# Loads of fold factors at the start of a graph-network kernel, and the place of a fold's last split quarter

## The chip, the cores and the metric

The kernel runs on one core of a Trainium2 chip. The time is that of the device in microseconds, from the launch of the program to its end. A core has a matrix engine (PE, TensorE), three engines for elementwise work (DVE, the vector engine; ACT, the scalar engine; POOL, GpSimd), and SP, which issues transfers (DMAs). Each runs its own list of instructions in order, and they wait for each other by semaphores. Tiles lie in SBUF with up to 128 partitions; matmuls write to PSUM (`ps`), which has eight banks.

## What is computed

The reference takes 625 nodes with 512 features and 20625 edges and runs four graph layers. Cut to what matters here:

```python
    # layer L1: three rounds of mean aggregation in both directions
    for l in range(3):
        h_self = h
        fwd_neigh = _mean_agg(h, src, dst, n) @ W_fwd[l].T
        bwd_neigh = _mean_agg(h, dst, src, n) @ W_bwd[l].T
        cat = jnp.concatenate((h_self, fwd_neigh, bwd_neigh), axis=1)
        h = jax.nn.relu(cat @ W_self[l].T)
...
    # layer L0, over all edges (sorted by the kernel first)
    edge_feature = jax.nn.silu(edge_rbf @ We1 + be1) @ We2 + be2
    msg = edge_feature * x[col]
    agg = jax.ops.segment_sum(msg, row, num_segments=N_NODES)
```

In L1, `W_fwd[l]` and `W_bwd[l]` are each followed by a 512-column part of `W_self[l]`, with nothing but a matrix product between. The kernel multiplies these weights together beforehand: three rounds with two directions make six products of two 512x512 matrices, the fold products.

## The kernel before

**Stages.** The first 140 us or so prepare two things side by side. One is the six fold products (`FOLDS` = 6). The other is a sort of the edges into slots of 128 by the chunk of their source node. Then the edge loop of layer L0 runs (83 steps), and then the node layers. The prediction speaks of the first part and of the start of the edge loop.

**A fold product.** Product m has the factors `fold_a[m]` and `fold_b[m]`, 1 MB each, loaded by `load_factors(m)` on SP into the tile `stage0` or `stage1`, by turns (m % 2). The product has four quarters (m,0) to (m,3), each with its own PSUM bank: `fold(m, u)` on PE. ACT copies each quarter out (`product_out`, line L695, tile `folded`), and SP stores the whole product to memory (`save_product`).

The first three products (m < `WHOLE` = 3) are taken straight from `stage` in float32: 8 records of about 0.43 us each (L1050). The last three are split first. ACT rounds a quarter of both factors to `fold_hi` (`factor_high`, L680), DVE takes the rest as `fold_lo` (`factor_low`, L1575), and PE runs three fast matmuls for each (L997 to L999). A quarter of the splitting is a quarter of the summed index, and every quarter (m,u) of the product sums over all four. So (m,0) needs all four splits, one after the other, and the others need none that is new. `stage0`, `fold_hi0` and `fold_lo0` lie in one region of SBUF, those with number 1 in another.

**The sorting columns.** The sort is a scatter by matmul. There are 28 groups of columns, each with 6 columns (the last has 3). For each group DVE builds `hot_lo`, `hot_hi` (L1563) and `ended` (L1569), ACT builds `keyed` (`mark`, L688) out of `hot_lo`, and PE adds them up (`place`, L1035 and L1038). The tiles of a group form a ring of four, so a group waits until PE is done with the one four before.

**What sets the order.** It is written out by hand. The table `AFTER[m][u]` gives the groups that PE places behind `fold(m, u)`: one or two behind each from (1,0) to (3,3), none behind (4,1) and later. ACT and DVE walk through the same quarters. In the step of (m,u) they first do the columns of the groups that PE needs behind the next quarter, then split quarter u of the factors of product m + 1, and ACT then copies out (m,u). In (2,1) the layer norm of x lies between, and in (4,1) the tables of the sort.

**The queue of SP.** The transfers go out in the order of the code, with waits between. Factors m + 2 can be loaded when product m no longer reads the buffer: m = 2, 3, 4 wait for PE (`fold_mm`), and m = 5 waits for the splitting of product 3 (`split_lo`). Between stand the stores of the products and of `h32` (the normed input, to `h_dram`), and the weights of the edge loop.

**Behind the products.** When the last quarter of product 5's factors is split, DVE still does the low half of the edge weights (`we_lo`, L1582), tables (L1587 to L1646), `rT_lo` (L1654), two memsets (L1720, L1721) and `s_lo` (L1660). PE runs the edge loop's first matmuls between and behind (5,2) and (5,3).

## Time and profile before

| | us |
|---|---|
| median of 3 runs | 1199.06 |
| the three runs | 1197.98, 1199.06, 1199.83 |
| the profiled execution | 1200.69 |
| its span, first to last instruction | 1198.9 |
| PE busy | 1158.1 (97% of the span) |
| DVE busy | 851.5 (71%) |
| ACT busy | 680.5 (57%) |
| mean granted clock of PE | 0.989 |

The profiled execution is one run of the program; all durations are from it. A line of a timeline gives the start, the time taken, engine, line, operation, the output and input tiles with their shapes, and in brackets how long the engine had stood still and what released it. Several instructions of a kind in a row are one line (x6). Times are counted from the start of the span. Matmuls overlap, so a matmul's own duration is longer than the distance between two starts.

### The profile page before, as it was taken

What the parts mean: (1) busy time and instruction counts of PE and PEld (TensorE: products, weight loads), DVE (VectorE), ACT (ScalarE), POOL (GpSimd) and SP (SyncE); (2) the same over time, 40 slices, a digit from 0 to 9 for tenths busy, and PEclk for the clock granted to TensorE, in tenths of its full rate; (3) what the DMA queues carried; (4) which work ended last, traced back from release to release, by engine and by line L of the source; (5) the groups of instructions that cost most, each with busy time, mean ns of one, the idle gap of its engine ahead of it and who ended that gap; (6) DMA issues with size and microseconds to landing.
All of it is one profiled execution on the core that took longest, in us unless ns stands there. A gap on an engine that the chain in (4) does not pass through costs nothing.

```text
span 1198.9 us, 20918 instructions
## 1 busy us (share of the span) xinstructions
PE 1158.1 (97%) x6268; PEld 970.2 (81%) x6268; DVE 851.5 (71%) x1479; ACT 680.5 (57%) x1351; POOL 418.6 (35%) x546
## 2 busy tenths in 40 slices
PE   6989899999999999999999999998899999999997
PEld 3658788888888888888888888886789888798786
DVE  8767777777777777777777777777977234175664
ACT  3567567676676766767676676765734223142352
POOL 2001555565546555555555555551500000001000
PEclk9999999999999999999999999999899999999999
DMA  5544622222222222222222322221101202022101
GB/s 192 205 154 158 234 87 72 83 82 71 87 74 79 80 74 85 70 85 77 76 85 68 87 74 79 82 72 36 44 1 37 71 8 97 0 71 71 44 2 44
DMA packets 26966, 95.88 MB, mean 80 GB/s; under 512 B 6533, under 2 KB 6783, under 8 KB 22578
## 3 DMA queue, kind: packets, MB, share of 16 engines
q0 software_dynamic: 18592, 54.42, 15.2%
q1 hardware_dynamic: 8208, 40.84, 9.5%
q8 instruction: 23, 0.38, 0.1%
q10 hardware_dynamic: 130, 0.13, 0.0%
q14 instruction: 13, 0.11, 0.0%
HBM read 86.52 MB, written 8.85 MB: 80 GB/s over the span
## 4 chain that ended last, share of the span: by engine, by line
PE 88%; DVE 6%; ACT 3%; issue 1%; DMA 1%; DVEq 0%; SPq 0%; ACTq 0%
PE ps L1004 13%; PE ps L1006 12%; PE ps L1005 12%; PE ps L997 9%; PE ps L999 9%; PE ps L998 9%; PE ps L1012 3%; PE ps L1011 3%; PE ps L1111 3%; PE ps L1110 3%; PE ps L1050 3%; PE ps L1115 2%; PE ps L1038 1%; PE ps L1247 1%; PE ps L1065 1%
## 5 line engine op out<-in xcount | busy, mean ns | idle before, releaser
L1004 PE MATMUL ps<-we_hi,s_hi 128*128 128x512 f32 x664 | 268.7, 405 | 0.0
L1006 PE MATMUL ps<-we_hi,s_lo 128*128 128x512 f32 x664 | 260.2, 392 | 0.0
L1005 PE MATMUL ps<-we_lo,s_hi 128*128 128x512 f32 x664 | 260.1, 392 | 0.0
L578 POOL DMA_INDIRECT xg<-h_dram,node_picks x166 | 177.0, 1066 | 96.7 <-POOL node_picks L568 66.1
L720 ACT ACTIVATE m_hi<-msg 128x512 fp32r<-128x512 f32 x166 | 105.0, 632 | 156.9 <-DVE msg L1667 92.9
L572 POOL DMA_INDIRECT rbf<-in_edge,edge_picks x166 | 171.5, 1033 | 50.5 <-issue 33.5
L1672 DVE TENSOR_TENSOR m_lo<-msg,m_hi 128x512 fp32r<-128x512 f32 x166 | 114.9, 692 | 59.3 <-ACT m_hi L720 58.6
L1660 DVE TENSOR_TENSOR s_lo<-s,s_hi 128x1024 fp32r<-128x1024 f32 x83 | 101.8, 1226 | 75.5 <-ACT s_hi L714 50.3
L1006 PEld LDWEIGHTS ps<-we_hi,s_lo 128*128 128x128 f32 x664 | 124.9, 188 | 28.6
L1005 PEld LDWEIGHTS ps<-we_lo,s_hi 128*128 128x128 f32 x664 | 125.7, 189 | 21.1
L1004 PEld LDWEIGHTS ps<-we_hi,s_hi 128*128 128x128 f32 x664 | 125.3, 189 | 21.4
L710 ACT ACTIVATE s<-ps,be 128x256 f32<-128x256 f32 x332 | 129.6, 478 | 2.9 <-PE ps L999 2.9
L1667 DVE TENSOR_TENSOR msg<-ps,xg 128x512 f32<-128x512 f32 x166 | 113.5, 684 | 0.0
L997 PE MATMUL ps<-rT_hi,we_hi 128*128 128x256 f32 x332 | 102.7, 309 | 3.8 <-issue 2.7
L723 ACT ACTIVATE ps<-row_a 128x512 f32<-128x512 f32 x166 | 97.0, 584 | 0.1
L999 PE MATMUL ps<-rT_hi,we_lo 128*128 128x256 f32 x332 | 94.3, 284 | 0.0
L998 PE MATMUL ps<-rT_lo,we_hi 128*128 128x256 f32 x332 | 94.2, 284 | 0.0
L714 ACT ACTIVATE s_hi<-s 128x1024 fp32r<-128x1024 f32 x83 | 88.0, 1061 | 5.6
L630 POOL TENSOR_TENSOR diag<-adj_hi,adj_lo 125x125 f32<-125x125 f32 x5 | 2.1, 456 | 213.7 <-DVE w_lo L1901 213.7
L1702 DVE TENSOR_TENSOR acc_agg<-ps,acc_agg 125x512 f32 x80 | 55.3, 692 | 22.5 <-issue 22.0
L568 POOL COPY node_picks<-slot_dst 128x2 int32 (+1 forms) x83 | 15.2, 183 | 160.6 <-DVE msg L1667 160.6
L997 PEld LDWEIGHTS ps<-rT_hi,we_hi 128*128 128x128 f32 x332 | 63.8, 192 | 4.6 <-issue 3.1
(301 smaller groups left out, 2556.4 us busy)
## 6 DMA issues: line engine op xcount, KB each, us to landing
stage<-in_fold_a SPq DMA_DIRECT2D x6, 1024.0 KB, 5.1
stage<-in_fold_b SPq DMA_DIRECT2D x6, 1024.0 KB, 8.6
fold_dram<-folded SPq DMA_DIRECT2D x6, 1024.0 KB
wstage<-fold_dram SPq DMA_DIRECT2D x6, 1024.0 KB, 4.9
w_raw<-in_nodew SPq DMA_DIRECT2D x3, 1024.0 KB, 7.2
wstage<-in_selfw SPq DMA_DIRECT2D x3, 1024.0 KB, 5.0
rbf<-in_edge,edge_picks POOLq DMA_INDIRECT x166
xg<-h_dram,node_picks POOLq DMA_INDIRECT x166
```

Of the source, the lines that this page charges most:

```text
L572: pool.indirect_dma_start(rbf[t.slot][:, j], None, a["edge"], bass.IndirectOffsetOnAxis(ap=edge_picks[t.slot][:, j:j + 1], axis=0)).then_i ...
L578: pool.indirect_dma_start(xg[t.slot][:, j], None, h_dram, bass.IndirectOffsetOnAxis(ap=node_picks[t.slot][:, j:j + 1], axis=0)).then_inc(x ...
L710: act.activation(s32[:, u], ps[:, 1 + u // 2, (u % 2) * PAIR:(u % 2) * PAIR + PAIR], ACT.Silu, bias=be1[:, u:u + 1]).then_inc(silu_ready, 1)
L720: act.activation(m_hi[s][:, j], msg[j][:], ACT.Copy).then_inc(m_hi_ready, 1)
L997: pe.matmul(outp, lh, rh, start=start, stop=False)
L998: pe.matmul(outp, lh, rl, start=False, stop=False)
L999: return pe.matmul(outp, ll, rh, start=False, stop=stop)
L1004: pe.matmul(outp, lh, rh, start=False, stop=False, skip_group_check=True)
L1005: pe.matmul(outp, lh, rl, start=False, stop=False, skip_group_check=True)
L1006: return pe.matmul(outp, ll, rh, start=False, stop=False, skip_group_check=True)
L1667: dve.tensor_tensor(msg[j][:], ps[:, 3 + j], xg[s][:, j], op=ALU.mult).then_inc(msg_ready, 1)
L1672: dve.tensor_tensor(m_lo[s][:, j], msg[j][:], m_hi[s][:, j], op=ALU.subtract).then_inc(m_lo_ready, 1)
```

## The change

The factors of products 0, 1 and 2 no longer go to `stage`. They go to three tiles `plain0` to `plain2`, which take the places of `fold_hi1`, `fold_lo1` and `fold_hi0`; these are written only when products 0, 1 and 2 are done. `stage` is left to products 3, 4 and 5. SP issues the loads of products 0 to 4 at the start, with x between 1 and 2, and there is a semaphore for each product's load. The load of 5 still waits for the splitting of product 3, but now stands in front of the stores of `h32` and of products 2 and later. `factor_high` waits for `fold_mm` in every product that is split.

The second part moves the split of the last quarter (u == K - 1). On ACT and on DVE it now stands in front of the columns of that step, where it stood behind them.

```diff
+        plain_at = (spare.at - 2 * 2 * K * F * 4, spare.at - 2 * K * F * 4, pre.at - 2 * 2 * K * F * 4)
+        plain = [Region(at)(f"plain{m}", [P, 2, K, F], F32) for m, at in enumerate(plain_at)]
...
-        stage_in = [sem(f"stage_in{i}") for i in range(2)]
+        stage_in = [sem(f"stage_in{m}") for m in range(FOLDS)]
...
             def load_factors(m):
+                factors = plain[m] if m < WHOLE else stage[m % 2]
                 for part, w in enumerate((a["fold_a"], a["fold_b"])):
-                    sp.dma_start(stage[m % 2][:, part].rearrange("p k f -> p (k f)"), w[m]).then_inc(stage_in[m % 2], 16)
+                    sp.dma_start(factors[:, part].rearrange("p k f -> p (k f)"), w[m]).then_inc(stage_in[m], 16)
...
             load_factors(0)
             load_factors(1)
             sp.dma_start(x_res[:], a["x"].rearrange("(c p) f -> p c f", p=NC)).then_inc(x_in, 16)
-            sp.wait_ge(fold_mm, K)
-            load_factors(2)
+            for m in range(2, FOLDS - 1):
+                load_factors(m)
             save_product(0)
...
-            for m in range(3, FOLDS):
-                if m - 2 < WHOLE:
-                    sp.wait_ge(fold_mm, K * (m - 1))
-                else:
-                    sp.wait_ge(split_lo, K * (m - 1 - WHOLE))
-                load_factors(m)
-                save_product(m - 2)
-                if m == 4:
-                    sp.wait_ge(ln_act, 1 + C)
-                    sp.dma_start(h_dram.rearrange("(c p) f -> p c f", p=NC), h32[:]).then_inc(h_saved, 16)
-            for m in range(FOLDS - 2, FOLDS):
+            save_product(1)
+            sp.wait_ge(split_lo, K)
+            load_factors(FOLDS - 1)
+            sp.wait_ge(ln_act, 1 + C)
+            sp.dma_start(h_dram.rearrange("(c p) f -> p c f", p=NC), h32[:]).then_inc(h_saved, 16)
+            for m in range(2, FOLDS):
                 save_product(m)
...
             def factor_high(m, k):
-                act.wait_ge(stage_in[m % 2], 32 * (m // 2 + 1))
-                if m - 2 >= WHOLE:
-                    act.wait_ge(fold_mm, K * (m - 1))
+                act.wait_ge(stage_in[m], 32)
+                act.wait_ge(fold_mm, K * (m - 1))
...
             for n, (m, u) in enumerate(units):
+                if u == K - 1 and WHOLE <= m + 1 < FOLDS:
+                    factor_high(m + 1, u)
                 if n + 1 < len(units):
                     for i in AFTER[units[n + 1][0]][units[n + 1][1]]:
                         mark(i)
-                if WHOLE <= m + 1 < FOLDS:
+                if u < K - 1 and WHOLE <= m + 1 < FOLDS:
                     factor_high(m + 1, u)
...
-                        mm = pe.matmul(ps[:, 1 + u], stage[m % 2][:, 0, k, f], stage[m % 2][:, 1, k],
+                        mm = pe.matmul(ps[:, 1 + u], plain[m][:, 0, k, f], plain[m][:, 1, k],
...
+                if u == K - 1 and WHOLE <= m + 1 < FOLDS:
+                    factor_low(m + 1, u)
                 if n + 1 < len(units):
                     for i in AFTER[units[n + 1][0]][units[n + 1][1]]:
                         hots(i)
                 if (m, u) == (FOLDS - 2, 1):
                     slot_tables()
-                if WHOLE <= m + 1 < FOLDS:
+                if u < K - 1 and WHOLE <= m + 1 < FOLDS:
                     factor_low(m + 1, u)
```

On SP, the transfers from the first factors to the load of product 5 stand in this row before (`stage_134` and `stage_135` are stage0 and stage1, `folded_196` and `folded_197` the two tiles of finished products):

```order
3 L470 DMA stage_134<-in_fold_a 128x2048
4 L470 DMA stage_134<-in_fold_b 128x2048
5 L470 DMA stage_135<-in_fold_a 128x2048
6 L470 DMA stage_135<-in_fold_b 128x2048
7 L478 DMA x_res<-in_x 125x5x512
8 L470 DMA stage_134<-in_fold_a 128x2048
9 L470 DMA stage_134<-in_fold_b 128x2048
10 L474 DMA fold_dram<-folded_196 128x2048
...
20 L474 DMA fold_dram<-folded_196 128x2048
21 L495 DMA h_dram<-h_82 125x5x512
22 L470 DMA stage_135<-in_fold_a 128x2048
23 L470 DMA stage_135<-in_fold_b 128x2048
```

Of the change (`plain_140` to `plain_142` are plain0 to plain2, `folded_199` and `folded_200` the tiles of finished products):

```order
7 L482 DMA x_res<-in_x 125x5x512
8 L474 DMA plain_142<-in_fold_a 128x2048
9 L474 DMA plain_142<-in_fold_b 128x2048
10 L474 DMA stage_135<-in_fold_a 128x2048
11 L474 DMA stage_135<-in_fold_b 128x2048
12 L474 DMA stage_134<-in_fold_a 128x2048
13 L474 DMA stage_134<-in_fold_b 128x2048
14 L478 DMA fold_dram<-folded_199 128x2048
...
20 L474 DMA stage_135<-in_fold_a 128x2048
21 L474 DMA stage_135<-in_fold_b 128x2048
22 L494 DMA h_dram<-h_82 125x5x512
23 L478 DMA fold_dram<-folded_199 128x2048
```

The loads of products 3 and 4 have moved up behind that of 2, and the last load has moved in front of `h_dram` and the store of product 2.

On ACT, the steps of (2,2) and (2,3), where groups 17 to 20 are keyed and the last two quarters of product 3's factors split, before:

```order
34 L688 ACTIVATE keyed_189<-hot_lo_181,keys 125x256 x3
35 L688 ACTIVATE keyed_190<-hot_lo_182,keys 125x256 x3
36 L680 ACTIVATE fold_hi_137<-stage_135 128x2x512
37 L695 ACTIVATE folded_196<-ps 128x512
38 L688 ACTIVATE keyed_191<-hot_lo_183,keys 125x256 x3
39 L688 ACTIVATE keyed_188<-hot_lo_180,keys 125x256 x3
40 L680 ACTIVATE fold_hi_137<-stage_135 128x2x512
41 L695 ACTIVATE folded_196<-ps 128x512
```

And in the change:

```order
34 L686 ACTIVATE keyed_192<-hot_lo_184,keys 125x256 x3
35 L686 ACTIVATE keyed_193<-hot_lo_185,keys 125x256 x3
36 L678 ACTIVATE fold_hi_137<-stage_135 128x2x512
37 L693 ACTIVATE folded_199<-ps 128x512
38 L678 ACTIVATE fold_hi_137<-stage_135 128x2x512
39 L686 ACTIVATE keyed_194<-hot_lo_186,keys 125x256 x3
40 L686 ACTIVATE keyed_191<-hot_lo_183,keys 125x256 x3
41 L693 ACTIVATE folded_199<-ps 128x512
```

The second `fold_hi` has moved from behind the two `keyed` to in front of them; the same is done on DVE with `fold_lo`, and on both once more in the step of (3,3).

## Rows read from the trace of the kernel before

**Rows 1.** The page: busy time of each engine, share of the span, instructions.

```profile
PE 1158.1 (97%) x6268; PEld 970.2 (81%) x6268; DVE 851.5 (71%) x1479; ACT 680.5 (57%) x1351; POOL 418.6 (35%) x546
```

**Rows 2.** Waits, 0 to 140 us: waiting <- waited for: total us, times, longest.

```profile
PE ps L997 <- DVE fold_lo L1575: 4.4, 1, 4.4
...
PE ps L997 <- issue: 2.7, 1, 2.7
...
PE ps L997 <- DVE rT_lo L1654: 1.1, 1, 1.1
```

**Rows 3.** Timeline of PE: group 17, then starts in (3,0) to (4,0).

```profile
78.48 0.24 PE L1035 MATMUL ps<-hot_hi,keyed 125*128 125x166 f16 x1 [0.51 <-issue]
...
81.14 0.48 PE L997 MATMUL ps<-fold_hi 128*128 128x512 f32 x1
...
87.90 0.80 PE L997 MATMUL ps<-fold_hi 128*128 128x512 f32 x1 [4.44 <-DVE fold_lo L1575]
...
92.81 0.48 PE L997 MATMUL ps<-fold_hi 128*128 128x512 f32 x1
...
103.82 0.48 PE L997 MATMUL ps<-fold_hi 128*128 128x512 f32 x1
...
109.32 0.48 PE L997 MATMUL ps<-fold_hi 128*128 128x512 f32 x1
...
111.47 0.39 PE L997 MATMUL ps<-fold_hi 128*128 128x512 f32 x1
```

**Rows 4.** Timeline of ACT: first split of product 3, and around its last.

```profile
63.54 1.06 ACT L680 ACTIVATE fold_hi<-stage 128x1024 fp32r<-128x1024 f32 x1 [4.82 <-DMA stage<-in_fold_b]
...
80.42 0.58 ACT L695 ACTIVATE folded<-ps 128x512 f32<-128x512 f32 x1
...
84.34 1.30 ACT L688 ACTIVATE keyed<-hot_lo,keys 125x256 f16<-125x256 f16 x3 [0.69 <-DVE hot_lo L1563]
85.55 1.04 ACT L680 ACTIVATE fold_hi<-stage 128x1024 fp32r<-128x1024 f32 x1
```

**Rows 5.** Timeline of DVE: the splits of product 3, and the columns between.

```profile
80.55 1.22 DVE L1575 TENSOR_TENSOR fold_lo<-stage,fold_hi 128x1024 fp32r<-128x1024 f32 x1 [3.54 <-ACT fold_hi L680]
81.70 0.55 DVE L1563 TENSOR_TENSOR hot_lo<-iota_lo,lo 125x768 f16<-125x768 f16 x1
...
83.69 0.55 DVE L1563 TENSOR_TENSOR hot_lo<-iota_lo,lo 125x768 f16<-125x768 f16 x1
...
86.62 1.23 DVE L1575 TENSOR_TENSOR fold_lo<-stage,fold_hi 128x1024 fp32r<-128x1024 f32 x1 [0.85 <-ACT fold_hi L680]
87.76 0.55 DVE L1563 TENSOR_TENSOR hot_lo<-iota_lo,lo 125x768 f16<-125x768 f16 x1
```

**Rows 6.** Busy time by stretch; last three columns: PE's clock, DMA share, GB/s.

```profile
15.00:18.00 3.00, 3.00 (x7) 1.27 (x7) 2.93 (x5) 1.10 (x1) 0.00 (x0) 1.00 0.33 128
82.00:90.00 8.00, 3.56 (x15) 2.35 (x14) 7.15 (x14) 5.34 (x11) 0.00 (x0) 0.85 0.60 244
...
131.00:145.00 14.00, 11.33 (x56) 9.56 (x56) 8.64 (x9) 8.80 (x16) 6.71 (x7) 0.88 0.64 232
```

**Rows 7.** DMA issues: loads of folds 0, 1, 2, 5 (second halves); last, us to landing.

```profile
stage<-in_fold_b SPq DMA_DIRECT2D x1, 1024.0 KB, 7.4
...
stage<-in_fold_b SPq DMA_DIRECT2D x1, 1024.0 KB, 11.4
...
stage<-in_fold_b SPq DMA_DIRECT2D x1, 1024.0 KB, 8.7
...
stage<-in_fold_b SPq DMA_DIRECT2D x1, 1024.0 KB, 12.9
```

**Rows 8.** Timelines of ACT and DVE: copy of (4,2), last split quarter of product 5.

```profile
118.55 0.60 ACT L695 ACTIVATE folded<-ps 128x512 f32<-128x512 f32 x1 [0.84 <-PE ps L999]
...
120.13 1.23 DVE L1575 TENSOR_TENSOR fold_lo<-stage,fold_hi 128x1024 fp32r<-128x1024 f32 x1 [1.16 <-ACT fold_hi L680]
```

**Rows 9.** Timeline of SP: issue of fold 1's second half.

```profile
2.91 0.64 SPq L470 DMA_DIRECT2D stage<-in_fold_b  x1
```

More of the change, by code:

```diff
@@ L298, in build @@
         assert spare.at <= keep.at
+        plain_at = (spare.at - 2 * 2 * K * F * 4, spare.at - 2 * K * F * 4, pre.at - 2 * 2 * K * F * 4)
+        plain = [Region(at)(f"plain{m}", [P, 2, K, F], F32) for m, at in enumerate(plain_at)]
+        assert len(plain) == WHOLE
         ends16 = pre("ends16", [EP, 2, ETP], F16)
@@ L1044, in fold @@
                 if m < WHOLE:
-                    pe.wait_ge(stage_in[m % 2], 32 * (m // 2 + 1))
+                    pe.wait_ge(stage_in[m], 32)
                 if m > 0:
```

## The prediction

> **Notation.** (m,u) is quarter u of fold product m. "Group i" is the i-th of 28 groups of sorting columns. A quarter of a fold's factors is split by fold_hi on ACT and then fold_lo on DVE. Only the first 140 us of 1198.9 us matter; I take the later work as it is and shift it.
>
> **What bounds the kernel now.** I read the page's busy times first [rows 1]: PE is busy 97% of the span, so a gain is either PE work removed or PE idle time removed. The change removes no matmul. So I went to the waits of the first 140 us [rows 2] and looked for PE's idle time: 4.4 us in which a split matmul waited for fold_lo, 1.1 us for rT_lo, and 2.7 us of "issue". (What PE waits at the start for the counting of edges is not touched.)
>
> PE's timeline shows the big hole [rows 3]. (3,0) starts at 81.14 and could run its fourth quarter 2.15 us later (111.47-109.32, the same distance in (4,0)); it runs it at 87.90. A smaller hole, 0.51 us, lies in front of group 17 at 78.48. What came late is seen on ACT and DVE [rows 4, 5]: the fourth quarter's fold_hi ran at 85.55, behind groups 19 and 20 (the latter keyed at 84.34), and its fold_lo at 86.62 to 87.85. The granted clock of 82 to 90 us is 0.85 [rows 6]. So part of it ran at the lower of its two levels (1.2 instead of 2.4 GHz), behind a PE that had stood still for 4.4 us.
>
> Farther back, ACT started fold_hi of product 3's first quarter at 63.54, having stood still 4.82 us for the factors, so since 58.72 [rows 4]: they are issued only when PE has let go of their buffer. From there on DVE and ACT take 6.07 us for two groups and one quarter (81.70 to 87.76 [rows 5]), and everything they do hangs on that start.
>
> **Part 1, early loads.** The factors of folds 0 to 2 lie in places of their own and those of 3 and 4 are issued at the start. The bytes are the same, 2 MB a fold. The loads land one after the other, not together: fold 1's second half, issued at 2.9 us [rows 9], lands 11.4 us later at 14.3; fold 0's, issued a microsecond before it, takes 7.4 us, so it lands some 5 us sooner; that of fold 2 takes 8.7 us [rows 7]. So 2 MB more in the queue land 5 us later, 2.4 us a megabyte and at worst 8.7/2 = 4.4, and what stands behind does not slow what stands in front. x_res comes next; while it moves, the DMA share is 0.33 at 128 GB/s [rows 6], so its 1.25 MB take 10 us, to about 24 us. The 6 MB behind it take 6 x 2.4 = 14 us, 26 at worst: all there by 38 to 50 us. Needed: fold 3 at 58.7, fold 2 a few us sooner, fold 4 not before 84. All is covered, at cost 0. Whether so long a stretch of transfers slows DVE or ACT this trace does not show apart; hot_lo takes 0.55 us at 81.70, shortly behind a load, and at 87.76, during one [rows 5], so I take nothing.
>
> The gain: ACT starts (3,0)'s fold_hi at 58.72 instead of 63.54, 4.8 us sooner, and DVE and ACT keep that lead to (2,2), since nothing else holds them there. The added wait for fold_mm is no wait: ACT has by then copied out the product that it asks for. PE gets 0.51 us at once: group 17, for which it waited until 78.48 [rows 3], is ready, so (3,0) starts at 81.14-0.51 = 80.63.
>
> **Part 2, the last quarter in front of the columns.** The third quarter's fold_lo, 80.55 to 81.78 before, moves to 75.7 to 76.9. ACT's next fold_hi, the last quarter's, now runs right behind folded (80.42 before, 75.6 now), at 76.1 to 77.1, and fold_lo at 77.1 to 78.4. PE wants that quarter at 80.63+2.15 = 82.8. So the hole goes. What is pushed back: groups 19 and 20 start 1.3 us behind, at 78.4 instead of 77.0, yet 3.3 us before their 81.70. A group takes DVE 2.0 us and is keyed 1.95 us behind its start (84.34+1.30 less 83.7), so group 20 is ready at 82.3; PE wants it at 80.63+2.8+1.36 = 84.8 (2.8 for the matmuls of a quarter of the product, 1.36 for a group: 5.50 a unit, 103.82 to 109.32 [rows 3]). From group 21 on no split stands between, so DVE is 5.4 us ahead of before; with 6.07 us a unit against PE's 5.50 it loses 0.57 us a unit on PE, three times: group 24 is ready at 92.4 where PE wants it at 95.8. The same turn comes in (3,3): group 21 starts at 82.4, the third quarter's fold_lo ends 3 x 6.07 us later at 100.6, the last one's at 102.1, PE wants it at 104.8; group 27 is ready at 104.0, wanted at 105.4. Nothing waits. Without part 2 the first place would be 87.85-4.8 = 83.0 against 82.8 and the second 87.76-4.8+3 x 6.07+2.0+0.9+1.2 = 105.3 against 104.8: beside part 1, part 2 is worth only some 0.2 to 1 us.
>
> **The sum.** Hole before group 17: 0.51. Hole in (3,0): 87.90 less (81.14+2.15) = 4.61. Low clock behind it: from 87.90 to (3,1) at 92.81 are 4.91 us; the same work at full clock takes 5.50-2.15 = 3.35; the difference is 1.56 [rows 3]. Together **6.7 us**: (3,1) at 86.1 instead of 92.81.
>
> For the clock term: 0.85 over 8 us is 2.4 us at half speed up to 90 us, and some more behind. The Trainium skill (TensorE: Matmul & The Clock Gate, "What's actually happening") says that the gate's timing does not start with the kernel, so that the same stall can meet more or less of it. By that the sum would run from 5.1 to 6.7 us; the trace has one sample and I take it.
>
> **Where the 6.7 us go next.** PE runs (3,1) to (4,3) without a wait. The last fold_hi of all stands in ACT's list right behind folded of (4,2) at 118.55, which PE released, and DVE's last fold_lo at 120.13 waits for it [rows 8]. So it moves with PE. Behind it DVE works nearly without a break (we_lo, tables, memsets, s_lo, rT_lo), and PE's last holes, 1.1 us and 2.7 us [rows 2], are waits for that DVE work. It hangs on that fold_lo, so both holes stay and move by 6.7 us. Their low clock (0.88 from 131 to 145 us [rows 6]) stays too. Then the edge loop begins, where PE is the bound.
>
> Two queues are passed. SP: the factors of fold 5 are now issued in front of the stores of h and of product 2. Before, the load stood behind h and took 12.9 us to landing [rows 7]. Now it is issued at 78.5 and with the 8.7 us of fold 2 there by about 87. h then takes 10 us as x did, to 97, and product 2's store, 1 MB, lands near 100; ACT overwrites that buffer in (4,0) at 109.32+2.8-6.7 = 105.4. Five us of cover; if it were late, ACT would wait that much, and with it (5,3). POOL's gathers wait for the tables and move along; h is there long before.
>
> 1200.69 us of the profiled execution (span 1198.9) less 6.7 is 1194.0; it stands 1.6 us above the median of the three runs. Against that median: 1199.06-6.7 = **1192.4 us**.
>
> **Rivals.**
>
> A, the columns set PE's pace. For: 6.07 against 5.50 us a unit, and a cover of only 2.5 us at group 20 and 1.5 us at group 27. If the early start of ACT were lost altogether (part 2 alone), group 26, ready at 87.76+2 x 6.07+2.0+1.95 = 103.8 before, is 1.3 us later and (4,0) starts at 105.1+1.4 = 106.5 instead of 109.32: 2.8 us gained, 1196.3. Half of the lead lost gives some 5 us, 1194. The late store of product 2 is of the same size. Against: every wait I could follow has cover.
>
> B, the gain is given back before the edge loop: (5,3)'s chain hangs on something that does not move. For: the load of fold 5 took 12.9 us [rows 7] and landed shortly before its use. Against: it is now issued 9 us sooner. If so the time is that of before, 1199.
>
> C, slower: the queued loads share the engines. Fold 0's second half landed near 9.4 (14.3 less 5), a little before PE's first fold matmul, so a delay of some 1 us decides. If the 6 MB more took turns with it, fold 0 would be there by 25 to 35 us instead of 9.4; even a tenth of that share, 2.5 us, would be 1.5 us at the start, and full sharing costs 15 to 25 us less the 6.7 us won: 1207 to 1217. Against: the landings 5 us apart, with both folds and x queued, which sharing would put together.
> The Trainium skill (DMA: Bandwidth & Descriptors, "Queues, rings and completion order") says that a later descriptor may finish its write before an earlier one, so completion in order isn't promised. By that C could occur; by the rows its cost is 0.
>
> D, the change doesn't act as written: fold_mm in front of fold_hi held ACT back. For product m it asks for product m - 2, all of which ACT itself has copied out by then. I give it nothing.
>
> **How the numbers follow.** Forecast 0.78 (1190.5 to 1194.5: the runs of before spread from 1197.98 to 1199.83, 1 us either way, and the clock term may be missing or be somewhat larger). A 0.12 (1194 to 1196.5). B 0.06. C 0.04. The range 1190.0 to 1196.5 leaves out B and C. A measurement here tells about 0.2% (2.4 us) from no change: faster 0.90 (forecast and A), same 0.06, slower 0.04.
>
> **What would show it.** fold_hi's first instruction near 58.7 us with no wait for a DMA; PE without a hole near 83 us and its granted clock 1.00 from 82 to 90 us; (3,1) near 86.1; the fourth quarter's fold_lo near 77 us; the two holes near 123 and 131 us of the same size; PE's first fold matmul at its old place, near 10.4 us. I am wrong if PE waits for columns between 84 and 106 us, if ACT waits for a store near 105, or if low clock appears at another place.

## The result, and the profile after

The change takes 1190.91 us in the median of 4 runs (1190.32 to 1191.46), the kernel before 1199.27 us beside it (4 runs, 1197.98 to 1199.83). The ratio is 0.9935, with a 95% interval of 0.9922 to 0.9948: 8.4 us, or 0.65%, faster. Timed again on another chip (`after_again`, below) it took 1192.02 us against 1197.66: 5.6 us, ratio 0.9952 (0.9939 to 0.9966). Before that second timing I had expected 6.7 to 7.5 us if the surplus of the first was luck of single executions, and 8.4 us or more if the change made it. It came out below both; the prediction of 6.7 us lies between the two timings. One run of `fold3_store` (below) took 1916 us at a granted clock of 0.56 and is left out of its median.

The profiled execution of the change took 1190.32 us, with a span of 1188.5 against 1198.9. PE is busy 4.7 us less [rows 1] with as many matmuls, so some of them ran faster; where is told below. Busy time of each engine, from the page of the change:

```profile
PE 1153.4 (97%) x6268; PEld 969.4 (82%) x6268; DVE 850.0 (72%) x1479; ACT 680.2 (57%) x1351; POOL 422.8 (36%) x546
```

The waits of 0 to 140 us, as in [rows 2] (waiting <- waited for: total us, times, longest). The 4.4 us wait for `fold_lo` is gone from PE, and nothing has taken its place. The two waits near the edge loop stand as they did:

```profile
DVE fold_lo L1575 <- ACT fold_hi L678: 11.7, 11, 3.5
...
PE ps L997 <- issue: 2.7, 1, 2.7
...
PE ps L997 <- DVE rT_lo L1656: 1.1, 1, 1.1
```

The timeline of PE, as in [rows 3]: group 17, (3,0), its fourth quarter, (3,1), (3,3), (4,0). The fourth quarter now follows the start of (3,0) by 2.16 us, with no bracket behind it:

```profile
76.53 0.24 PE L1035 MATMUL ps<-hot_hi,keyed 125*128 125x166 f16 x1
...
79.19 0.47 PE L997 MATMUL ps<-fold_hi 128*128 128x512 f32 x1
...
81.35 0.39 PE L997 MATMUL ps<-fold_hi 128*128 128x512 f32 x1
...
84.72 0.48 PE L997 MATMUL ps<-fold_hi 128*128 128x512 f32 x1
...
95.76 0.48 PE L997 MATMUL ps<-fold_hi 128*128 128x512 f32 x1
...
101.25 0.48 PE L997 MATMUL ps<-fold_hi 128*128 128x512 f32 x1
```

The timeline of ACT, against [rows 4]: the first split of product 3 with no wait for a DMA, the last one right behind the copy, and groups 19 and 20 behind that:

```profile
57.35 1.04 ACT L678 ACTIVATE fold_hi<-stage 128x1024 fp32r<-128x1024 f32 x1
...
74.22 0.58 ACT L693 ACTIVATE folded<-ps 128x512 f32<-128x512 f32 x1
74.70 1.05 ACT L678 ACTIVATE fold_hi<-stage 128x1024 fp32r<-128x1024 f32 x1
77.57 1.31 ACT L686 ACTIVATE keyed<-hot_lo,keys 125x256 f16<-125x256 f16 x3 [1.82 <-DVE hot_lo L1563]
79.57 1.31 ACT L686 ACTIVATE keyed<-hot_lo,keys 125x256 f16<-125x256 f16 x3 [0.68 <-DVE hot_lo L1563]
```

The timeline of DVE, against [rows 5]: the last quarter's `fold_lo`, 10.8 us sooner, and the columns behind it:

```profile
75.79 1.23 DVE L1575 TENSOR_TENSOR fold_lo<-stage,fold_hi 128x1024 fp32r<-128x1024 f32 x1 [0.20 <-ACT fold_hi L678]
76.93 0.55 DVE L1563 TENSOR_TENSOR hot_lo<-iota_lo,lo 125x768 f16<-125x768 f16 x1
```

Busy time by stretch, as in [rows 6] (then PE's clock, DMA share, GB/s). In 82 to 90 us the granted clock is 1.00 where it was 0.85:

```profile
82.00:90.00 8.00, 8.00 (x82) 7.29 (x82) 7.14 (x14) 5.29 (x12) 0.00 (x0) 1.00 0.65 239
```

The DMA issues of 20 to 60 us and 70 to 100 us, against [rows 7] (KB, us from issue to landing). The first line is the last of the early loads, product 4's second half; then the load of product 5, and the store of product 2:

```profile
stage<-in_fold_b SPq DMA_DIRECT2D x1, 1024.0 KB, 26.4
...
stage<-in_fold_b SPq DMA_DIRECT2D x1, 1024.0 KB, 8.2
fold_dram<-folded SPq DMA_DIRECT2D x1, 1024.0 KB, 17.3
```

And the timeline of SP around them, against [rows 9]. `plain<-in_fold_a` at 4.08 is an issue that itself lasted 11.55 us:

```profile
4.08 11.55 SPq L474 DMA_DIRECT2D plain<-in_fold_a  x1
...
19.65 1.18 SPq L474 DMA_DIRECT2D stage<-in_fold_b  x1
...
77.04 0.33 SPq L474 DMA_DIRECT2D stage<-in_fold_a  x1
77.41 0.43 SPq L474 DMA_DIRECT2D stage<-in_fold_b  x1
```

**Where the 10.4 us between the two spans lie.** I took the start of the same matmul in both traces, place by place:

| start of | before | after | difference | gained since the row above |
|---|---|---|---|---|
| (0,0), first fold matmul | 10.36 | 10.36 | 0 | |
| (2,0) | 55.80 | 54.53 | -1.27 | 1.27 |
| (3,0) | 81.14 | 79.19 | -1.95 | 0.68 |
| (3,0), fourth quarter | 87.90 | 81.35 | -6.55 | 4.60 |
| (3,1) | 92.81 | 84.72 | -8.09 | 1.54 |
| (4,0) | 109.32 | 101.25 | -8.07 | 0 |
| the matmul behind the 2.7 us hole | 138.08 | 130.00 | -8.08 | 0 |
| a matmul of the edge loop, near 800 us | 799.96 | 790.32 | -9.64 | 1.56 |
| the last matmuls | 1192.35 | 1182.70 | -9.65 | 0 |

Three things add up to the 9.65 us of the last row, and the change made only the middle one; the other 0.8 us of the 10.4 lie behind the last matmuls (6.6 against 5.8 us to the end of the span) and I did not follow them. The first 1.27 us arise in the first fold matmuls, at the start of the program. From 9 to 22 us PE runs one kind of matmul back to back in both kernels, and gets through 21 in one trace and 24 in the other (first line before, second after):

```profile
10.36 12.03 PE L1050 MATMUL ps<-stage 128*128 128x512 f32 x21
```

```profile
10.36 12.04 PE L1050 MATMUL ps<-plain 128*128 128x512 f32 x24
```

PE begins at half pace, and full pace came 2.6 us sooner in the one execution. Busy time of 12 to 16 us shows the same, 6 matmuls against 9 (the clock column, third from the end, reads 1.00 in both, but only because the trace has no record of the clock yet: the first one, at full speed, begins at 16.0 us before and at 13.4 us in the change, just when the pace doubles):

```profile
12.00:16.00 4.00, 4.00 (x6) 1.69 (x5) 3.89 (x17) 0.00 (x0) 0.00 (x0) 1.00 0.51 207
```

```profile
12.00:16.00 4.00, 4.00 (x9) 1.81 (x8) 3.89 (x17) 0.38 (x1) 0.00 (x0) 1.00 0.52 209
```

Half the pace for 2.6 us more is a loss of 1.3 us, the 1.27 of the table. It is no effect of the change: `order_only`, which has the loads of before, shows (2,0) at 54.53 too, and `loads_only`, which has those of the change, at 55.78. Third, 1.6 us build up behind the last hole, nearly all of it (1.3) evenly in the edge loop, in which nothing was changed: in 150 to 350 us, with a PE that is busy all the time, it is 1054 matmuls against 1056 (before, then after):

```profile
150.00:350.00 200.00, 200.00 (x1054) 169.14 (x1053) 154.16 (x265) 139.03 (x292) 113.00 (x146) 1.00 0.26 79
```

```profile
150.00:350.00 200.00, 200.00 (x1056) 169.52 (x1055) 155.35 (x268) 139.16 (x292) 119.86 (x144) 1.00 0.27 79
```

In all fourteen traces, the one stretch of the edge loop from a matmul near 150 us to the one near 800 us takes either 650.0 us (before, `fold2_first`, `order_again`, `store_later`) or 648.7 us (the ten others), a pace that differs by 0.2%. `order_only` and `order_again`, one and the same kernel, have one each. So this belongs to the execution, and the trace of before has the slower pace.

What is left, from (2,0) to the matmul behind the last hole, is 82.28 us before and 75.47 us after: **6.8 us**, or 6.65 if the 0.2% of pace is taken off before's. In the experiments I use this distance beside the time. It leaves out the start and the edge loop, and it came out alike to 0.2 us wherever the same code was profiled twice.

### The profile page after: what moved, and what is told of

Read it like the earlier page. It is cut to its first block, busy times and chain, and to the rows that moved or that the text cites. A ratio compares the mean times of both kernels' runs of the same rounds, so it can differ in the third digit from the quotient of the medians.

```text
span 1188.5 us, 20926 instructions
## 1 busy us (share of the span) xinstructions
PE 1153.4 (97%) x6268; PEld 969.4 (82%) x6268; DVE 850.0 (72%) x1479; ACT 680.2 (57%) x1351; POOL 422.8 (36%) x546
## 4 chain that ended last, share of the span: by engine, by line
PE 91%; DVE 5%; ACT 2%; issue 1%; DMA 0%; DVEq 0%
PE ps L1004 13%; PE ps L1006 12%; PE ps L1005 12%; PE ps L997 9%; PE ps L998 9%; PE ps L999 9%; PE ps L1050 4%; PE ps L1012 3%; PE ps L1011 3%; PE ps L1111 3%; PE ps L1110 3%; PE ps L1038 2%; PE ps L1115 2%; PE ps L1035 1%; PE ps L1247 1%
```

## Experiments

All kernels, with the interval of the ratio to the kernel before, timed beside it on the same chip. The first four rows are of one chip, the next four of another, the last four of a third, so medians of different groups are compared by what each gained on its own before. "Distance" is the one just defined, before: 82.28. The last column says whether a stretch at 1.2 GHz lies directly behind it.

| kernel | median us (runs) | before | ratio (95%) | distance | slow stretch |
|---|---|---|---|---|---|
| `loads_only` | 1193.02 (5) | 1198.29 | 0.9955 (0.9942 to 0.9969) | 76.21 | yes |
| `order_only` | 1195.89 (11) | 1198.29 | 0.9979 (0.9970 to 0.9988) | 79.23 | no |
| `filled_hole` | 1196.05 (11) | 1198.29 | 0.9978 (0.9969 to 0.9987) | 81.25 | no |
| `fold2_first` | 1196.04 (11) | 1198.29 | 0.9980 (0.9970 to 0.9990) | 75.48 | yes |
| `after_again` | 1192.02 (5) | 1197.66 | 0.9952 (0.9939 to 0.9966) | 75.47 | yes |
| `stores_first` | 1191.93 (5) | 1197.66 | 0.9951 (0.9938 to 0.9965) | 75.47 | yes |
| `tables_early` | 1189.24 (5) | 1197.66 | 0.9930 (0.9917 to 0.9944) | 74.04 | yes |
| `fold3_late` | 1193.46 (5) | 1197.66 | 0.9962 (0.9948 to 0.9975) | 77.83 | no |
| `order_again` | 1195.35 (10) | 1198.27 | 0.9972 (0.9961 to 0.9983) | 79.43 | yes |
| `store_later` | 1194.02 (6) | 1198.27 | 0.9966 (0.9953 to 0.9980) | 77.90 | no |
| `fold3_again` | 1194.40 (6) | 1198.27 | 0.9969 (0.9957 to 0.9980) | 77.74 | yes |
| `fold3_store` | 1194.86 (8) | 1198.27 | 0.9970 (0.9959 to 0.9981) | 79.43 | yes |

### Each part alone

`loads_only` is the change without its second part:

```diff
-                if u == K - 1 and WHOLE <= m + 1 < FOLDS:
-                    factor_high(m + 1, u)
...
-                if u < K - 1 and WHOLE <= m + 1 < FOLDS:
+                if WHOLE <= m + 1 < FOLDS:
                     factor_high(m + 1, u)
```

and the same for `factor_low`. 

> The early loads alone; the last quarter is split behind the columns, as before. My account (the early loads give the lead of 4.8 us, the new place of the last quarter only 0.2 to 1 us beside it): 0.2 to 1 us slower than the whole change at 1190.9, so 1191.1 to 1191.9; in the trace a PE wait for fold_lo of some 0.2 us in (3,0) and 0.5 us in (4,0). The rival (the order does the work, since it takes the split out from behind the columns): a gain over before of less than 3 us, 1196 or more, with a hole of over 3 us left in (3,0).

The distance is 76.21, 0.74 us more than the change's and inside the "0.2 to 1 us" of the prediction. The wait that comes back on PE, in its waits of 0 to 140 us, is the one that was worked out:

```profile
PE ps L995 <- DVE fold_lo L1573: 0.2, 1, 0.2
```

In (3,0) the fourth quarter starts 2.53 instead of 2.16 us behind the first and (3,1) another 0.12 us later; in (4,0), the second place, (4,1) follows after 3.73 instead of 3.48 us. That is the 0.74. The early loads alone bring 6.1 us of the 6.8. Two of the numbers expected were off: of the 0.5 us of wait in (4,0) the trace shows less, no wait of its own and 0.25 us in all, and the median was 1193.02 us, above the 1191.1 to 1191.9. It is of another chip than the 1190.9 that the range was made from; it gained 5.3 us on its own before, where the change gained 8.4 and 5.6.

`order_only` is the kernel before with the second part alone. 

> The new place of the last quarter alone, loads as before. My account: fold_hi still starts at 63.5 us behind the transfer; the big hole in (3,0) falls to under 0.5 us, but DVE and ACT then set PE's pace with 6.07 us a unit, and of the 6.7 us some 2.8 us are left at (4,0): 1196.3 us, with PE waiting a half to one us for columns in each unit. The rival (the order does it all): 1191 to 1193. A third (nothing without the loads): 1199.

The hole in (3,0) is gone here too, yet the distance is 79.23: 3.05 us gained and not 6.8. ACT still stands before its first split, and part of the lead that the order gives at (3,0) is lost again to the columns. The waits of 0 to 140 us:

```profile
ACT fold_hi L680 <- DMA stage<-in_fold_b: 4.6, 1, 4.6
...
PE ps L1037 <- DVE ended L1571: 2.4, 3, 1.1
```

So PE does wait for columns, as in rival A, but otherwise than expected: not in every unit, but for 1.11 and 0.48 us in (3,0) and 0.78 us behind (4,0), and the three units between run at some 5.5 us without a wait. Nor is A's sum borne out. It had 2.8 us left at (4,0); counted from (2,0) on, 4.3 us are left there (49.19 against 53.52 us), and only the third wait and a longer one for `rT_lo` (1.48 instead of 1.12 us) bring it down to 3.05. That the end comes near 2.8 is chance. The parts aren't additive (6.1 and 3.05 are more than 6.8): both remove the same hole, and only the early start of ACT keeps PE from the waits for columns.

### Is the clock behind the hole a cost of its own?

`filled_hole` is the kernel before with 18 matmuls more in front of the wait. They write to a PSUM bank whose content isn't used, and add nothing to the result:

```diff
+                        if (m, k) == (WHOLE, K - 1):
+                            for _ in range(18):
+                                pe.matmul(ps[:, 7], fold_hi[m % 2][:, 0, 0, f], fold_hi[m % 2][:, 1, 0], start=True, stop=True)
                         pe.wait_ge(split_lo, (m - WHOLE) * K + k + 1)
```

> The kernel before, with 18 matmuls into a PSUM bank that nobody reads (ps bank 7) in front of the wait for the last split quarter in (3,0); they fill 4.1 us of the 4.6 us hole and add nothing to the result. If the slow clock behind the hole is the price of PE's standing still, its granted clock stays 1.00 from 82 to 100 us and (3,1) starts 1.56 us sooner though nothing else is sooner: 1199.3 less 1.3 to 1.6, 1197.8. If the slow clock comes from something else in that part: same as before, 1199.3, or slower.

Busy time by stretch, first before, then `filled_hole` (PE first, its clock third from the end):

```profile
84.00:88.00 4.00, 0.10 (x1) 0.10 (x1) 3.15 (x6) 2.73 (x5) 0.00 (x0) 0.95 0.20 78
88.00:92.00 4.00, 4.00 (x28) 3.38 (x29) 3.83 (x8) 2.90 (x7) 0.00 (x0) 0.62 0.72 279
```

```profile
84.00:88.00 4.00, 3.82 (x17) 2.82 (x15) 3.14 (x6) 2.74 (x5) 0.00 (x0) 1.00 0.20 80
88.00:92.00 4.00, 3.81 (x40) 3.45 (x41) 4.00 (x9) 2.61 (x7) 0.00 (x0) 1.00 0.74 290
```

The real work started no sooner (the fourth quarter at 88.19 us instead of 87.90), but behind it PE ran 40 matmuls in 4 us instead of 28, and from (2,0) to (3,1) it took 35.72 instead of 37.01 us: 1.3 us for a clock that didn't fall. So the clock term is real, and separate from the wait. The median fell by 2.2 us, 0.6 more than the upper expectation. The trace does not explain the surplus: it is of the slowest of the eleven runs (1197.03 us), though the slow stretch behind the second hole was absent in it too, and that is the next point.

### The late hole: a slow stretch that comes or not

The last column of the table shows something that no kernel's edit explains. PE stands still 2.7 us (2.56 to 2.68) before the second group of edge matmuls in every kernel. In ten of the fourteen traces (before, the change, and the twelve runs here) the clock falls behind it, in four it doesn't. `order_only` and `order_again` are the same kernel. Their stretches from 134 to 140 us:

```profile
134.00:140.00 6.00, 6.00 (x34) 5.16 (x34) 2.78 (x5) 3.42 (x8) 2.35 (x4) 1.00 0.98 347
```

```profile
134.00:140.00 6.00, 5.09 (x22) 4.68 (x23) 1.87 (x6) 2.74 (x5) 3.18 (x3) 0.72 1.01 344
```

The matmuls behind the hole take 2.89 us without the stretch and 4.2 to 4.4 us with it: 1.3 to 1.5 us that one execution of a kernel pays and another does not. `fold3_late` and `fold3_again`, also one kernel, differ in the same way. The Trainium skill (TensorE: Matmul & The Clock Gate, "What's actually happening") says that the gate's timing does not start with the kernel; by that rule the same stall meets it or not, and these pairs agree, though no trace shows the gate's timing itself. In the prediction I used that sentence for the large hole only, where the stall was 4.4 us and the single trace had a fall.

### Does the queue serve the loads one by one?

`fold2_first` issues product 2's factors in front of product 0's:

```diff
+            load_factors(2)
             load_factors(0)
             load_factors(1)
```

> The change, with the 2 MB of fold 2's factors issued in front of fold 0's instead of behind x. If a queued transfer is served in its turn (my account), fold 0's second half lands 4.9 us later, at 14.3, and PE starts its first fold matmul 3.9 us later than at 10.4: 3.9 us slower than the change, 1194.8. If all queued loads share the engines (rival C of the prediction), fold 0's landing hardly depends on the order: 1190.9 to 1191.9.

The timeline of PE: the first fold matmul, 10.36 us in all other kernels, here:

```profile
14.44 2.04 PE L1051 MATMUL ps<-plain 128*128 128x512 f32 x2 [3.89 <-DMA plain<-in_fold_b]
```

2 MB in front cost 4.1 us, as expected of a queue that serves its transfers in turn. The rest of the kernel kept its distance (75.48). The median gained 2.25 us on its own before, where `after_again` gained 5.64: 3.4 us less, with 3.9 expected. So rival C, the loads sharing the engines, is refuted at the place where it would have cost time, the landing of product 0.

The first fold matmul at 10.36 us in the change does not show by itself that 6 MB behind cost nothing. When product 0's second half landed, near 9.5 us, SP still stood in the issue that lasted from 4.08 to 15.63; five of the six loads behind x were issued after it. And those loads did overlap. The DMA issues of 15.7 to 16.7 us in the change:

```profile
plain<-in_fold_b SPq DMA_DIRECT2D x1, 1024.0 KB, 20.5
stage<-in_fold_a SPq DMA_DIRECT2D x1, 1024.0 KB, 17.0
```

The first, product 2's second half, issued at 15.68, landed at 36.1; product 3's first half, issued behind it at 16.32, landed at 33.4. PE wanted product 2 at 54.5 us and product 3 was wanted later still, so it cost nothing here.

### The stores behind the load of product 5

`stores_first` puts the stores of product 2 and of h back in front of the last load:

```diff
+            save_product(2)
+            sp.wait_ge(ln_act, 1 + C)
+            sp.dma_start(h_dram.rearrange("(c p) f -> p c f", p=NC), h32[:]).then_inc(h_saved, 16)
             sp.wait_ge(split_lo, K)
             load_factors(FOLDS - 1)
-            sp.wait_ge(ln_act, 1 + C)
-            sp.dma_start(h_dram.rearrange("(c p) f -> p c f", p=NC), h32[:]).then_inc(h_saved, 16)
```

> The change with SP's old order in one place: the stores of product 2 and of h go out in front of the load of fold 5's factors. My account: the order costs nothing either way, since the load then lands by 101 us with its first use at 102.9, and in the change the store of product 2 has some 5 us of cover: same as the change within 0.5 us. If the new place of the load is part of the gain: 1 to 4 us slower than the change, with ACT waiting for a transfer near 103 us.

No difference: 1191.93 against 1192.02 us, and the distance is the same 75.47. The load landed 12.9 us after its issue instead of 8.2, and it was issued at 89.91 instead of 77.41; it was still in time (landed at 102.8, first split of product 5 at 104.2, with no wait). That part of the new queue order is worth nothing here.

### Taking the gain farther

`tables_early` moves the tables that don't depend on late data (`bucket_tables`, some 5 us of DVE: 116.01 to 121.01 us in the change) from behind `we_lo` into the step of (2,2), where the change has left DVE idle 3.5 us in front of a `fold_lo`:

```diff
+                if (m, u) == (2, 2):
+                    bucket_tables()
...
             weights_low(0, 1)
-            bucket_tables()
```

> The change, with the bucket tables of the sort (5.0 us of DVE work that depends only on the counts) computed in the step of (2,2), where DVE stands still 3.5 us, instead of behind the last split. My account (PE's two last holes, 1.1 and 2.7 us, are waits for the DVE work behind the last split): the first hole goes and the second falls to some 1.4 us, when ACT's silu is the last; edge-loop matmuls 2.6 us sooner, and if a hole of 1.4 us no longer brings the slow clock, 4.1 us sooner: 1187 to 1188.5 against 1190.9. The rival (the holes hang on ACT or on the gathers): same as the change, or slower by the 1.5 us by which the columns of groups 19 and on are pushed back.

1189.24 us, 2.8 us under `after_again` and the fastest kernel here. The first of the two late holes is gone. The second only changed its name, since `rT_lo` stands behind `s_lo`, which waits for ACT. The timelines of PE and DVE:

```profile
121.51 0.28 PE L997 MATMUL ps<-rT_hi,we_hi 128*128 128x256 f32 x1
...
128.66 0.36 PE L997 MATMUL ps<-rT_hi,we_hi 128*128 128x256 f32 x1 [2.56 <-DVE rT_lo L1657]
```

```profile
127.00 1.23 DVE L1663 TENSOR_TENSOR s_lo<-s,s_hi 128x1024 fp32r<-128x1024 f32 x1 [0.87 <-ACT s_hi L712]
128.14 0.42 DVE L1657 TENSOR_TENSOR rT_lo<-ps,rT_hi 128x256 fp32r<-128x256 f32 x1
```

So the expected fall of the second hole to 1.4 us did not come, and neither did the 2.6 us: with the tables gone it hangs on ACT's `s_hi`. The trace gives 1.43 us of distance; the other 1.4 us of the median are of the size of the clock's and the start's luck, and five runs don't settle them.

### How early must the loads be? A miss, and its cause

`fold3_late` keeps the change, but issues the loads of products 3 and 4 when product 1 is done, as before:

```diff
-            for m in range(2, FOLDS - 1):
-                load_factors(m)
+            load_factors(2)
             save_product(0)
...
+            sp.wait_ge(fold_mm, 2 * K)
+            for m in range(3, FOLDS - 1):
+                load_factors(m)
             save_product(1)
```

> The change, but the factors of folds 3 and 4 are issued only when product 1 is done (as fold 3 was before), with all else as in the change. My account: what counts of the early loads is that ACT need not wait for fold 3; fold_hi starts again at 63.5 us and the time is that of the order alone, 1196, within 0.7 us. The rival (the loads of folds 2 and 4 matter as well): between 1192 and 1195.

It was faster than that, 1193.46 us, inside the range that I had given to the rival (the early loads of products 2 and 4 matter as well). I had taken it for `order_only` under another name, and the distances say that it is 1.4 us shorter (77.83 against 79.23). The copy of product 1's last quarter on ACT marks the moment of the load's issue in both; the wait for the load ended 8.7 us later in `order_only` (53.36 to 62.04) and 7.3 us in `fold3_late` (54.97 to 62.29). What differs around the load is what is queued behind it: the store of product 1 in one, the load of product 4 in the other. Four runs on one chip tested that. `order_again` and `fold3_again` repeat the two. `store_later` is `order_only` with that store held back, `fold3_store` is `fold3_late` with it put right behind the load of product 3:

```diff
                 load_factors(m)
+                if m == WHOLE:
+                    sp.wait_ge(fold_mm, 2 * K + 2)
                 save_product(m - 2)
```

```diff
-            for m in range(3, FOLDS - 1):
-                load_factors(m)
+            load_factors(3)
             save_product(1)
+            load_factors(4)
```

> The same kernel as order_only (only the last quarter's split moved), timed again beside fold3_again on one chip. In the first trace product 3's factors were usable 8.7 us after ACT's last copy of product 1 (53.36 to 62.04) and 82.1 us passed from product (2,0) on PE to the edge loop's matmul behind the last hole (54.53 to 136.65). Theory S (the store of product 1, queued right behind the load, slows it): both again within 0.4 us, and the time 1.4 us above that of fold3_again. Rival T (the difference was chance of the execution or of the chip): times within 0.7 us of fold3_again's.

> The same kernel as fold3_late (loads of products 3 and 4 issued once product 1 is done, otherwise the change). In its first trace the factors were usable 7.3 us after the copy (54.97 to 62.29), and 80.7 us passed from (2,0) to the matmul behind the last hole. S: the same again, time near 1194.3, 1.4 us below order_again. T: either distance moves toward 8.7 and 82.1, and the two times agree within 0.7 us.

> order_only with the store of product 1 held back until PE has done two quarters of product 2, so that nothing is queued behind product 3's load. S: the load is usable 7.3 to 7.5 us after the copy instead of 8.7, the distance from (2,0) to the matmul behind the last hole is 80.7 to 81.0 instead of 82.1, and the time is 1.2 to 1.4 us below order_again. T: 8.7, 82.1 and the time of order_again.

> fold3_late with the store of product 1 issued between the loads of products 3 and 4, that is right behind product 3's. S: the load is usable 8.5 to 8.9 us after the copy instead of 7.3, the distance rises from 80.7 to 82.1, the time by 1.2 to 1.4 us over fold3_again. T: no difference to fold3_again. If T holds in both, the cause of the 1.4 us stays open.

| | behind the load stands | copy to first split | distance | median |
|---|---|---|---|---|
| `order_again` | a store | 54.31 to 63.23: 8.9 | 79.43 | 1195.35 |
| `fold3_store` | a store | 54.52 to 63.40: 8.9 | 79.43 | 1194.86 |
| `store_later` | nothing | 54.62 to 61.95: 7.3 | 77.90 | 1194.02 |
| `fold3_again` | a load | 53.46 to 60.70: 7.2 | 77.74 | 1194.40 |

The waits of ACT for the load, of `order_again` and then of `store_later`:

```profile
ACT fold_hi L680 <- DMA stage<-in_fold_b: 4.8, 1, 4.8
```

```profile
ACT fold_hi L682 <- DMA stage<-in_fold_b: 3.2, 1, 3.2
```

And what the DMA engines moved meanwhile (last two columns: share, GB/s), of the same two:

```profile
58.00:60.00 2.00, 2.00 (x18) 1.34 (x17) 0.52 (x2) 0.40 (x2) 0.00 (x0) 1.00 1.06 365
60.00:62.00 2.00, 2.00 (x26) 1.89 (x24) 0.00 (x0) 0.00 (x0) 0.00 (x0) 1.00 0.94 242
```

```profile
58.00:60.00 2.00, 2.00 (x14) 1.19 (x13) 0.83 (x2) 0.71 (x2) 0.00 (x0) 1.00 1.05 438
60.00:62.00 2.00, 2.00 (x30) 2.00 (x27) 0.00 (x0) 0.05 (x1) 0.00 (x0) 1.00 0.57 242
```

A 1 MB store queued right behind a 2 MB load makes the load land 1.6 us later: its second half takes 8.5 us from issue to landing instead of 6.9, its first half the same 4.7 to 4.9 in all four. A load behind it costs nothing. `store_later`, which loads product 2 as late as the kernel before, is as fast as the `fold3` pair, so the early load of product 2 isn't the cause. The change itself has one more such case: its load of product 5, with the store of h right behind, took 8.2 us, and the load of product 4 in the kernel before, with nothing behind, 7.0.

The two new kernels fall in with their theory in the wait and in the distance of the table. In the medians theory S had 1.2 to 1.4 us between the kernels. Between `order_again` and `store_later` there are 1.3 us, between `order_again` and `fold3_again` 1.0, between the `fold3` pair only 0.5. These differences settle nothing either way, as the runs of one kernel spread over 2.7 to 4.8 us.

The distance in these four expectations (82.1 and 80.7 us) is another than the table's: it ends at a matmul 18 further on, 2.9 us behind the hole when no slow stretch comes, and so takes that stretch in. Measured to there it was 83.8 in `order_again`, 83.9 in `fold3_store`, 82.2 in `fold3_again` and 80.8 in `store_later`. Only the last met its number; the other three had the slow stretch, which the traces behind the expectations lacked. The table stops short of it, a choice made after seeing the traces, and the waits of ACT don't depend on it. How a store behind holds up a load in front is not shown; the trace shows only the lower rate while both are queued, 365 against 438 GB/s from 58 to 60 us.

## Why the prediction was right

The trace of the change starts its work behind (2,0) 1.3 us sooner, by luck of the start, so each of the times named is compared after taking that off.

- **Start of ACT.** Predicted 58.7 for the first `fold_hi`, with no DMA wait: 57.35 + 1.3 = 58.6, and no wait.
- **Hole before group 17.** Predicted 0.51, gained 0.68.
- **Hole in (3,0).** Predicted 4.61, gained 4.60. The fourth quarter's `fold_lo` was to run from 77.1 to 78.4 and ran from 75.79 to 77.02, with the shift 77.1 to 78.3. Group 20 was to be keyed at 82.3; it was at 79.57 + 1.31 = 80.88, with the shift 82.2. No wait for columns appears, in either of the places where cover was 1.5 to 2.5 us.
- **Clock.** Predicted 1.56, gained 1.54, and `filled_hole` got 1.3 us of it without touching the wait.
- **Sum.** Predicted 6.67 up to (3,1), gained 6.82. The distance to the last hole is 6.81 shorter as well: the two late holes moved along and kept their 1.1 and 2.7 us, as the chain in [rows 8] said.
- **The loads.** Predicted all there by 38 to 50 us; the last landed at 19.65 + 26.4 = 46. They did not land one after the other, as the prediction had it: product 3's first half overtook product 2's second, which landed at 36.1. With 18 us of cover that was harmless. The load of product 5 was predicted at 87, it landed at 77.41 + 8.2 = 85.6, with the shift 86.9. The store of product 2 was predicted near 100 and landed at 81.38 + 17.3 = 98.7, with the shift 100.0. SP stood 11.55 us in one issue, which I hadn't foreseen; nothing behind it was needed soon.
- **Part 2's worth.** Predicted 0.2 to 1 us beside part 1, measured 0.74 in the distance. Alone I gave it 2.8 us at (4,0) (rival A); there it is 4.1 to 4.3, and by the last hole 2.85 to 3.05.

Three statements were too simple. That the loads land one after the other held for the first four and not for those behind x. "What stands behind does not slow what stands in front" held where a load stood behind. Behind the load of product 3 in the kernel before stood a store, its second half took 8.5 us as in `order_again`, and by the four runs 1.6 of the 4.82 us that ACT waited were the store's doing. The sum was not touched, because it was made from the time at which ACT could start and not from the speed of the load. And I put the uncertainty of the time at 1 us either way from the runs' spread. That is nearly what a pair of medians shows (the change gained 8.4 us once and 5.6 the other time, 6.8 by the trace), but I hadn't seen where it comes from: up to 1.6 us at the start, 1.3 to 1.5 us behind the late hole, and 1.3 us by the pace of the edge loop.

## What to carry to other kernels

A hole on the bounding engine is often the end of a lead lost long before. Follow it back to the first engine that stood still, here ACT for 4.8 us at 58.7, some 25 us before PE's hole began. Moving work closer to its reader, without removing that first wait, only brings the next wait forward (3 of 6.8 us gained), and the gains of the two fixes cannot simply be added.

Where one profiled execution is compared with another, take the distance between two matmuls around the change rather than the span: 10.4 us of span were 6.8 us of change. And when a load is waited for, look at what is queued behind it, not only in front.

## What the runs showed of the hardware

- A 1 MB store queued right behind a 2 MB load delays the load's landing by 1.6 us (from 7.3 to 8.9 us after the copy that precedes it), a load in its place by nothing (7.2).
- The same stall of PE, 2.6 to 2.7 us, was followed by a stretch at 1.2 GHz in ten traces and by none in four; two kernels that were profiled twice showed both. It costs 1.3 to 1.5 us when it comes.
- At the start of the program the float32 matmuls ran at half pace, and (2,0) came between 54.5 and 56.1 us in kernels that do the same on PE up to there, as the full pace began between 13.4 and 16.6 us. The granted clock from 12 to 16 us reads 1.00 all the same, because the trace has no record of the clock before that moment.
- With a PE that is always busy, the edge loop ran at one of two paces, 650.0 or 648.7 us for the same work, by the execution.
- One issue on SP lasted 11.55 us in the change, the eighth transfer of the kernel, behind 5.25 MB of loads issued since 1.57 us; in the kernel before one at 87.87 lasted 6.42 us. Whatever must be issued soon should not stand behind it.
- Loads on one queue landed in the order of issue, 2.5 us a megabyte, up to the fourth; two issued at 15.7 and 16.3 us, behind x, landed at 36.1 and 33.4.
